# Two item steps for each hop of a chain between VectorE and TensorE, one ring for gathered rows, and a routing stage cut into four parts

## What is computed

```python
h = layernorm(x)
feat_src = (h @ W_n).reshape(N, 8, 32)
e = (left[src] + right[dst] + em_e) / 3.0      # each the sum over t of a term times edge_attr_4
e = where(e > 0, e, 0.2 * e)
e_max = segment_max(e, dst); e_exp = exp(e - e_max[dst])
a = e_exp / segment_sum(e_exp, dst)[dst]
x = x + segment_sum(feat_src[src] * a, dst)
probs = softmax(layernorm(x) @ router_w.T); topk_probs, topk_idx = top_k(probs, 2)
x = x + sum over the two experts of gate * (silu(z @ w1.T) * (z @ w3.T)) @ w2.T      # z = layernorm(x)
```

## Time and profile before

| | us |
|---|---|
| median of 3 runs (lowest, highest) | 4222.88 (4213.70, 4223.18) |
| the profiled execution | 4178.57 |
| its span | 4177.0 |

### The profile page before, as it was taken

How to read it: one execution, slowest core, us unless ns; L and a number is a source line. 1 busy time by engine, 2 the same in 40 slices (tenths; PEclk the granted TensorE clock), 3 DMA queues, 4 the chain that set the end, 5 groups by cost and what they waited for, 6 DMA issues and landing times. The chain is left out here.

```text
span 4177.0 us, 59301 instructions
## 1 busy us (share of the span) xinstructions
PE 3178.8 (76%) x12650; PEld 2450.8 (59%) x12651; DVE 1978.3 (47%) x5334; ACT 1614.9 (39%) x3611; POOL 1857.7 (44%) x1906
## 2 busy tenths in 40 slices
PE   3532777777787777777777777777765899999997
PEld 1221666666666666666666666666554577777775
DVE  6730555555555555555555555555754122222221
ACT  2311544554444544544545444444432122222221
POOL 0005456666566665665666656566145111111111
PEclk9865667776667776677767767677755899999998
DMA  7734444444444444444444444446553312111113
GB/s 231 247 135 121 123 128 128 131 129 129 127 130 127 130 136 129 131 130 128 130 128 129 130 126 130 127 129 116 106 169 132 89 30 32 32 30 32 32 31 82
DMA packets 309415, 481.35 MB, mean 115 GB/s; under 512 B 161911, under 2 KB 237507, under 8 KB 300366
## 3 DMA queue, kind: packets, MB, share of 16 engines
q0 software_dynamic: 100848, 285.40, 27.9%
q1 hardware_dynamic: 206302, 192.99, 15.2%
q10 hardware_dynamic: 2000, 0.06, 0.0%
HBM read 408.52 MB, written 76.12 MB: 116 GB/s over the span
## 5 line engine op out<-in xcount | busy, mean ns | idle before, releaser
L809 POOL DMA_INDIRECT rows<-table,idx x1664 | 1574.3, 946 | 1089.9 <-issue 509.0
L852 PE MATMUL ps_acc<-rows,hot 128*128 128x264 f32 x3328 | 1315.2, 534 | 313.1 <-DVE acc L1140 229.2
L852 PEld LDWEIGHTS ps_acc<-rows,hot 128*128 128x128 f32 x3328 | 790.3, 262 | 455.5 <-issue 342.2
L1140 DVE TENSOR_TENSOR acc<-acc,ps_acc 128x264 f32 x832 | 356.3, 428 | 1004.2 <-PE ps_acc L852 523.6
L837 PEld LDWEIGHTS ps_term<-er,hot_t 128*128 128x128 f32 x3328 | 665.4, 259 | 239.4 <-issue 171.2
L837 PE MATMUL ps_term<-er,hot_t 128*128 x3328 | 618.9, 318 | 109.3 <-issue 57.1
L1126 DVE TENSOR_TENSOR rows<-rows,ps_p 128x512 f32<-128x512 f32 x832 | 566.0, 680 | 0.5 <-ACT ps_p L955 0.5
L944 ACT ACTIVATE hot<-iota_row,neg_rel 128x128 f32<-128x128 f32 x1664 | 545.4, 388 | 5.4 <-PE ps_acc L852 5.4
L1684 PE MATMUL ps_h<-w,acc 128*128 x1680 | 529.3, 458 | 0.5 <-ACT acc L1603 0.5
L1596 POOL DMA_INDIRECT x_dram<-acc,to x105 | 161.7, 1540 | 752.5 <-ACT acc L1612 752.5
L919 ACT COPY e_t<-ps_e 128x128 f32<-128x128 f32 x208 | 57.4, 276 | 961.3 <-remote 529.8
(11 more groups left out here) (262 smaller groups left out, 2955.5 us busy)
## 6 DMA issues: line engine op xcount, KB each, us to landing
dst_row<-rel_d SPq DMA_DIRECT2D x52, 1024.0 KB
rows<-table,idx POOLq DMA_INDIRECT x1664
rec<-rec_d SPq DMA_DIRECT2D x832, 24.0 KB
rec_d<-acc SPq DMA_DIRECT2D x16, 1050.0 KB
acc<-slots_x SPq DMA_DIRECT2D x105, 130.0 KB, 2.1
acc<-in_edge_attr_dram SPq DMA_DIRECT2D x16, 700.0 KB
wrow<-in_L_ffn_w_dram SPq DMA_DIRECT2D x16, 640.0 KB
table<-fo SPq DMA_DIRECT2D x49, 148.0 KB
```

The source lines that it names most:

```text
L809: pool.indirect_dma_start(rows[w][:, t, :], None, table, bass.IndirectOffsetOnAxis(ap=idx[w][:, t:t + 1], axis=0)).then_inc(gathered[w * Q ...
L852: last = pe.matmul(ps_acc[m % 2][:, 0:PW], hot[m // QI % 2][:, m % QI * G + j, :], rows[m // NI][:, tile_of(m % NI, j), 0:PW], start=(j == ...
L1140: dve.tensor_tensor(so_far, so_far, ps_acc[m % 2][:, 0:PW].rearrange("p (h d) -> p h d", h=HEADS), ALU.add).then_inc(added, 1)
```

## The change

It has two halves. In the edge loop each hop of the chain gets two item steps: VectorE's parts stand at (3,0), (3,2), (0,0), (0,2) and (1,0), TensorE's at (3,1), (3,3), (0,1) and (0,3), ScalarE's exponentials at (1,1). All lags behind the chain grow by four items, and the rows lie in one ring of 36 items instead of two batches of 16. `blk_i` and `start_i` share one tile, on two partitions. In the routing stage VectorE's work is cut into `sum_up`, `normal`, `choose` and `send`, in another order. The counts within a group come from a scan on VectorE, so that `places` has two products. The weights' loads are issued by ScalarE, two units are turned ahead of the first group, one in each group and seven behind the last.

```diff
-LAG = 18
-SUM_LAG = 20
-ADD_LAG = 21
+LAG = 22
+SUM_LAG = 24
+ADD_LAG = 25
+ROW_ITEMS = 36
...
-        blk_i = sb(edges_ctx, "blk_i", [1, ITEMS], I32)
-        start_i = sb(edges_ctx, "start_i", [1, ITEMS], I32)
+        item_i = sb(edges_ctx, "item_i", [33, ITEMS], I32)
+        blk_i, start_i = item_i[0:1, :], item_i[32:33, :]
...
-            rows = [sb(st, f"rows{w}", [P, BT, FD]) for w in range(2)]
+            rows = sb(st, "rows", [P, ROW_ITEMS * G, FD])
...
-                            after_apart(pool, acc_done, batches(i, w, NI, u - 2 * NI + 1))
+                            k = batches(i, w, NI, u)
+                            after_apart(pool, acc_done, k - ROW_ITEMS + 1)
                             for j in range(G):
                                 t = tile_of(u, j)
-                                pool.indirect_dma_start(rows[w][:, t, :], None, table,
+                                pool.indirect_dma_start(rows[:, in_ring(k) + j, :], None, table,
                                                         bass.IndirectOffsetOnAxis(ap=idx[w][:, t:t + 1], axis=0)).then_inc(
                                                             gathered[w * QUADS + u // QI], 16)
...
-                                if v == QUADS - 1 and is_batch(i, w):
-                                    (turn_scores, item_ends, carries, back)[u](i, w)
+                                if v == QUADS - 1 and u == 1 and is_batch(i, w):
+                                    turn_scores(i, w)
+                                if v == QUADS - 1 and u == 3 and is_batch(i, w):
+                                    item_ends(i, w)
+                                if v == 0 and u == 1 and is_batch(i, w, -1):
+                                    carries(*one_ahead(i, w))
+                                if v == 0 and u == 3 and is_batch(i, w, -1):
+                                    back(*one_ahead(i, w))
...
-                        in_rows = rows[1 - w][:, :, 0:PW].rearrange("p e (h d) -> p e h d", h=HEADS)[:, :, :, HDIM]
-                        act.activation(in_rows, weight[:, :, :], ACT.Exp, scale=1.0 / 3.0).then_inc(exp_ok, 1)
+                        at = in_ring(batches(i, w, NI, -NI))
+                        n = min(BT, ROW_ITEMS * G - at)
+                        for lo, hi, to in ((0, n, at), (n, BT, 0)):
+                            if lo < hi:
+                                in_rows = rows[:, to:to + hi - lo, 0:PW].rearrange("p e (h d) -> p e h d", h=HEADS)[:, :, :, HDIM]
+                                last = act.activation(in_rows, weight[:, lo:hi, :], ACT.Exp, scale=1.0 / 3.0)
+                        last.then_inc(exp_ok, 1)
...
-                            at3, s3, _ = quad(w, v, -4)
+                            at3, s3, _ = quad(w, v, -5)
                             for u in range(QI):
-                                at, m = item(w, v, u, -4 * QI)
+                                at, m = item(w, v, u, -5 * QI)
                                 if is_item(i, at):
                                     squares(i, at, m)
-                                if v == 0 and u == 1 and is_batch(i, w, -1):
+                                if v == 1 and u == 1 and is_batch(i, w, -1):
                                     exp_batch(i, w)
-                                if v == 0 and u == 2 and is_batch(i, w, -1):
+                                if v == 1 and u == 2 and is_batch(i, w, -1):
                                     scales(i, w)
                                 if v == 1 and u == 3 and is_batch(i, w):
                                     turn_penalties(i, w)
...
                         dve.wait_ge(dst_row_in[w], i * 16 + 16)
+                        after(dve, less_ok, batches(i, w, 1))
                         dve.tensor_tensor(first[:, :], dst_row[w][:, 0, 0:1], part[:, :], ALU.is_equal).then_inc(first_ok, 1)
...
-                        step(dve.tensor_tensor(z, z, rows[w][:, v * QT:(v + 1) * QT, PW:FD], ALU.add))
+                        at = in_ring(batches(i, w, NI, v * QI))
+                        step(dve.tensor_tensor(z, z, rows[:, at:at + QT, PW:FD], ALU.add))
...
-                                if v == 0:
-                                    if u == 0 and is_batch(i, w):
+                                if v == 0 and is_batch(i, w, -1):
+                                    if u == 0:
+                                        link(*one_ahead(i, w))
+                                    if u == 2:
+                                        tops(*one_ahead(i, w))
+                                if v == 0 and u == 3 and is_batch(i, w):
+                                    first_node(i, w)
+                                if v == 1 and u == 0:
+                                    if is_batch(i, w):
                                         relate(i, w)
-                                    if u == 0 and is_batch(i, w, -1):
+                                    if is_batch(i, w, -1):
                                         below_top(i, w)
-                                    if u == 2 and is_batch(i, w):
-                                        first_node(i, w)
...
                                         scores(i, w)
-                                    else:
-                                        (item_tops, link, tops)[u - 1](i, w)
+                                    if u == 2:
+                                        item_tops(i, w)
 
                     all_slots(slot)
```

The routing stage, cut to its order:

```diff
-                            if n + W_RING < 2 * EXPERTS:
-                                sp.wait_ge(w_ps, KC * (n + 1))
-                                load_weights(n + W_RING)
...
+                    def load_weights(n):
+
+                        w, full, to = (w1, w3)[n % 2], (HCH - 1) * P, wrow[n % W_RING]
+                        act.dma_start(to[:, 0:HCH - 1, :], w[n // 2, 0:full, :].rearrange("(c p) d -> p c d", p=P)).then_inc(wrow_in[n % W_RING], 16)
+                        act.dma_start(to[0:HLAST, HCH - 1, :], w[n // 2, full:HID, :]).then_inc(wrow_in[n % W_RING], 16)
...
+                        if n + W_RING < UNITS:
+                            load_weights(n + W_RING)
+
+                    for n in range(W_RING):
+                        load_weights(n)
                     root(0)
-                    copies(0)
-                    for n in of_group(0):
+                    for n in range(FIRST_UNITS):
                         keep_weights(n)
-                    for g in range(1, GROUPS):
-                        root(g)
-                        exps(g - 1)
+                    for g in range(GROUPS):
                         copies(g)
-                        for n in of_group(g):
-                            keep_weights(n)
-                    exps(GROUPS - 1)
+                        exps(g)
+                        if g + 1 < GROUPS:
+                            root(g + 1)
+                        keep_weights(unit_of(g))
+                    for n in last_units():
+                        keep_weights(n)
...
-                        pe.matmul(at, ones[:, :], tally[:, :].unsqueeze(1).to_broadcast(wide), start=False, stop=True).then_inc(slot_ps, 1)
+                        at = ps_s[:, 0:BC * EXPERTS].rearrange("p (e b) -> p e b", e=EXPERTS)
+                        pe.matmul(at, not_above[:, :], chosen[:, :, :], start=True, stop=False)
+                        pe.matmul(at, ones[:, :], so_far[g % 2][:, :, :], start=False, stop=True).then_inc(slot_ps, 1)
...
-                    turn(0)
-                    for b in range(1, BLOCKS + 1):
-                        if b % BC:
-                            turn(b)
-                        logits(b - 1)
-                        if b % BC == BC - 1 and b > BC:
-                            places(b // BC - 1)
-                        if b % BC == 0:
-                            for n in of_group(b // BC - 1):
-                                turn_weights(n)
-                            if b < BLOCKS:
-                                turn(b)
-                    places(GROUPS - 1)
-                    pe.wait_ge(tally_ok, GROUPS)
+                    for n in range(FIRST_UNITS):
+                        turn_weights(n)
+                    for g in range(GROUPS):
+                        turn(g * BC)
+                        for b in range(g * BC, (g + 1) * BC):
+                            if b + 1 < (g + 1) * BC:
+                                turn(b + 1)
+                            logits(b)
+                        turn_weights(unit_of(g))
+                        places(g)
                     pe.wait_ge(slot_used, GROUPS)
-                    pe.matmul(ps_s[:, 0:EXPERTS], ones[:, :], tally[:, :], start=True, stop=True).then_inc(count_ps, 1)
+                    pe.matmul(ps_s[:, 0:EXPERTS], ones[:, :], so_far[(GROUPS - 1) % 2][:, :, BC - 1], start=True, stop=True).then_inc(count_ps, 1)
+                    for n in last_units():
+                        turn_weights(n)
...
```

(41 more changed lines are left out.)

59 lines of the change are left out of this document (29 added, 30 removed).

## The result

The changed kernel takes 4126.08 us (4118.71 to 4132.09, 4 runs) beside 4220.23 us of the kernel before (4213.7 to 4223.18): 0.9778, with a 95% interval of 0.9757 to 0.9799. That is 94 us faster where 304 were forecast. The profiled execution of after has a span of 4125.6 us, near its median; that of before is 42 us under its own, so the two traces show only 51 of the 94 us.

What follows compares the result with a forecast made beforehand. No engine is full: the edge loop is bound by mutual waits, TensorE and VectorE holding each other, above GpSimd's floor of 40.0 us a batch. 4178.6 - 260 + 4 - 48 = 3874.6, plus 44.3 gives 3919 us; range 3710 to 4180.

Steps and rivals of the forecast that it cites:

- (1) The chain's gain: Edge loop: two steps a hop remove TensorE's waits at L861 and L869; batch 50.0 to 45.0 us, -260 us.
- the estimate by steps: Edge loop: if the five chain steps cost what others cost, 2.72 us each, a batch takes 43.5 us.
- Late completions: Edge loop: TensorE's completions seen late, VectorE idle up to 5.54 us; untouched by the edit, could take back the gain.
- rival B: Edge loop: time moves to late completions, adds wait longer, batch stays 49 to 50 us; 4130 to 4180 us, chance 0.08.
- (2) exp split: Edge loop: exp_batch issues two ScalarE activations for one where items wrap around the ring, 3 batches in 9; costs nothing.
- (4): Edge loop: first_node moves one step later and waits for less_ok of the batch before; free.
- (5): Edge loop: exp_batch, scales and relate move four steps; ScalarE is held as before, so the cost only moves.
- (3) ring and lag: Edge loop: work behind the chain lags four items more, ring 36 against 32, gathers 12 steps ahead; nothing gained or lost.
- (6) the longer way through the steps: Edge loop's tail: four more steps without edge terms, at most 1.34 us each; +4 us.
- The clock: TensorE in the edge loop: mean granted clock kept at 0.71 in the forecast.
- Rival A: Edge loop: clock rises, GpSimd's 40.0 us becomes the bound, batch 41.5 us; 3737 us in all, chance 0.22.
- The stage, -48: Routing stage behind the loop: groups 19.5 us apart instead of 29.5, next stage starts at 3200 not 3248.9; -48 us.

Runs made afterwards that it cites:

- L: Condition of a run, not a change: TensorE's results are reported late; the kernel before takes 4206 to 4223 us.
- P: Condition of a run, not a change: none of the transposes checked is reported late; the kernel before takes 3613 to 3627 us.
- before_2: The kernel before, unchanged, run again in the prompt condition: 3618.3 us, beside 3617.9 us.
- after_3: The changed kernel, run again in the prompt condition: 3577.9 us, 0.987 of the kernel before.
- ring32: The changed kernel with a ring of rows of 32 items instead of 36, late condition: 4132.9 us, 0.979 of the kernel before.
- stage_only: The kernel before with only the changes behind the edge loop, prompt condition: 3569.6 us, 0.987 of the kernel before.
- half_3: The changed kernel with one gather an item instead of two behind the first 36 items, late condition: 3459.1 us, kernel before 4206.2.

## Why the prediction was right or wrong

The direction held, and 4126 lies in the range; the forecast of 3919 was too low by 207 us. By the traces the loop's term is 232 us short, the stage's 14, the longer way 5, and the last stage took 1 more, 253 in all. Against that stand 46 us that luck gave back: the forecast kept the 44.3 us between the profiled execution of before and the median, and in the changed kernel there is no such distance (4127.28 and 4126.08).

**(1) The chain's gain, -260: wrong.** The waits at L861 and L869 did go, 162.5 to 27.9 us; the 36.7 us before L837, which the sum took along, did not (39.3). The step that failed is the next one, which turned waits into time (4.15 us a batch "with nothing followed on", then 5.0): on L the adds give TensorE 271.9 us of new waits, and the loop of 2558.2 us becomes 27.8 shorter. Two things were wrong with it. Without any late report and without gathers the respacing is worth 1.1 us a batch, as the engines' other waits fill what it leaves; the estimate by steps (43.5) was worse still, since it priced the five chain steps as if their own work (two scans of 0.69 us in one step) weren't there. And on L the batch goes from 50.1 to 49.8 us, with its adds in step with the runs of gathers and their late reports. That these took what was left is argued from the one stretch and the counts; the loop without gathers was never run on L.

**Late completions** were named as "what is late next", and rival B was their account: loop at 49 to 50 a batch, time moved from TensorE's queue to VectorE's waits, 4130 to 4180. Its loop (49.8) came true, and its time within 4 us (4126), and it had 0.08. Its path did not: VectorE's waits before its adds grew by 20 us, TensorE's own for the adds by 272. The argument against it, that the chain's waits are on TensorE's own queue and nothing fills them, is the sentence that failed. The rows had said otherwise: 5.54 us behind a record that had ended, 491.3 us of waits for sums, and, left out of the rows, 268.1 us more of them and 457.9 us of ScalarE's, both put down to "remote", and a wait of 47.90 us at the head of the loop.

**(2) exp split, (4), (5):** no cost is seen: on P the loops of before_2 and after_3 take 2073.3 and 2072.9 us. But GpSimd is the bound there and would hide a small one. **(3) ring and lag:** nothing in the loop; ring32 bears it out on L. **(6) the longer way through the steps:** it shows at the head. The first add comes 9.1 us later; 3.6 of these lie ahead of the first gather (314.0 against 310.4), and the other 5.5 are four steps of about 1.4 us, near the 1.34 of the forecast. On P they are 8.2.

**The clock** was kept at 0.71 and is 0.76. As on P (0.82 to 0.84), it rose and gave the loop nothing, because TensorE was not what it waited for. **Rival A's** floor is real: GpSimd's 40.0 us are the bound of both kernels on P. GpSimd's wait of 326.0 us was read too low: with "remote" it was 484.8.

**The stage, -48:** on P -50.0 by the traces (237.6 to 187.6 us from the last add to the next stage) and 48.8 by stage_only; on L -33.6. Groups come 17.7 us apart on P where 19.5 was said (the forecast's 2 us for gaps of chained steps was too much). On L they are 17.6 to 23.9 apart and the last 37.2. The stage after, on L (28 scatters of L1306 go on without a rest from 3105 to 3142):

```profile
3129.37 0.37 ACT L1357 COPY xt<-ps_t 128x256 f32<-128x256 f32 x1 [7.43 <-remote]
...
3140.65 0.37 ACT L1357 COPY xt<-ps_t 128x256 f32<-128x256 f32 x1 [10.91 <-remote]
...
3146.30 0.75 ACT L1357 COPY xt<-ps_t 128x256 f32<-128x256 f32 x2 [5.28 <-remote]
...
3149.82 0.21 DVE L1497 TENSOR_REDUCE den<-ps_l 128x7 f32<-128x56 f32 x1 [25.18 <-PE ps_l L1411]
```

ScalarE waits 7.43, 10.91 and 5.28 us for transposes whose records had ended, and VectorE 25.18 us for the last group's logits behind them. On P the longest wait of ScalarE for these transposes is 2.0 us. So the same thing, beside another run of indirect DMAs, very likely costs the stage most of the 16 us by which it wins less on L than on P.

What would have shown it was mostly well chosen (no waits at L861 and L869, and "If VectorE's waits for sums grow by what TensorE's fall, it is B"). But it did not look like B: it is TensorE's wait for the adds that grew. GpSimd was to wait under 6 us a batch for sums; it waits 531 us in 48 batches, 11.1.

## What to carry to other kernels

A wait that is removed is worth what is left of it once the next wait has taken its share: sum an engine's waits before and after, and price by a version in which the other bounds are gone. Add up all rows of a wait, those put down to "remote" and "issue" too. Where an engine is shown waiting for a record that ended microseconds ago, the time may belong to something outside both engines; until that is named, a rival in which it eats the whole gain deserves a large chance, not 0.08. And a gain in a loop that two conditions bound differently (one by GpSimd, one by late reports) has to be weighed for each.

## What was not expected of the hardware

The same kernel runs at 4216 and at 3618 us with the same instruction durations, and which of the two it is changed between measurements under one chip number. In the slower condition TensorE's semaphores are released late while GpSimd issues gathers without a rest: up to 8.7 us behind the record's end in the loop, 43.6 us while the ring fills. In after, of 122 transposes that began 6 to 8 us into a run, all were late, and their reports came 1.9 us (median) behind the run's end, which is when the data of a gather has landed. Pauses are not the whole story, since in the routing stage two reports (at 3129.37 and 3140.65) came in the middle of a run. With one gather an item it vanishes from the loop. On P an unbroken run of 1664 gathers does nothing of the kind. SyncE's own short register instructions are slow on L too: 206 of 1088 took over 0.5 us in after (520 to 2200 us), none of 1340 in after_3, and 27 of 1440 in half_3. Together with the semaphore updates that the L traces lack, this suggests that something common to the engines is congested there; what, and whether recording has a part in it, no run here shows. A schedule that rests GpSimd without costing 0.84 us a time is what I would try next.

A small fill between gathers, with a wait for it, delays the next gather by 0.84 us against 0.30. With a VectorE operand moved from PSUM to SBUF and a third bank for sums, the gathers took 6% longer (948 to 1006 ns).
